# A mixture-of-experts block: the period loop written out, and expert weights requested ahead of their rows

## The reference

```
h = h + attn(layernorm(h))
x = layernorm(h)
topk_vals, topk_idx = top_k(x @ gate_w + gate_b, 2)
topk_w = softmax(topk_vals)
expert_out = relu(x @ w1[e] + b1[e]) @ w2[e] + b2[e]     # 16 experts, 64 -> 128 -> 64
h = h + layernorm(x + sum_k topk_w[k] * expert_out[topk_idx[k]]) * gamma + beta
```

## Time and profile before

| what | value |
|---|---|
| median of 3 runs | 4752.04 us (4744.88 to 4759.59) |
| profiled execution, its own time | 4752.51 us |
| its span, first to last instruction | 4750.7 us |
| mean granted TensorE clock | 0.839 |
| busy: PE, DVE, ACT, POOL | 77%, 63%, 46%, 70% |
| a steady period | 272.1 to 282.4 us |
| DMA over the span | 895.94 MB, mean 189 GB/s |

### The profile page before, as it was taken

How to read it: one execution, slowest core, us unless ns; L and a number is a source line. 1 busy time by engine, 2 the same in 40 slices (tenths; PEclk the granted TensorE clock), 3 DMA queues, 4 the chain that set the end, 5 groups by cost and what they waited for, 6 DMA issues and landing times.

```text
span 4750.7 us, 94109 instructions
## 1 busy us (share of the span) xinstructions
PE 3648.8 (77%) x24896; PEld 3139.7 (66%) x24896; DVE 3015.8 (63%) x9660; ACT 2167.0 (46%) x5266; POOL 3313.9 (70%) x3217
## 2 busy tenths in 40 slices
PE   4686887878778777877878887887878788788842
PEld 2565766767667676766767676775767677676732
DVE  1485858576684857767575775858577585767512
ACT  2354554444445444444544454454454445444401
POOL 0776777777677767777677776767777776777353
PEclk9888888888889888888988888898888978888855
DMA  7759584865848477584857758485774848562422
GB/s 238 247 154 273 160 266 132 253 190 181 244 126 267 131 234 218 164 256 119 258 146 238 222 161 246 125 262 148 221 237 141 259 125 267 151 177 58 120 66 62
DMA packets 922887, 895.94 MB, mean 189 GB/s; under 512 B 123866, under 2 KB 804442, under 8 KB 922200
## 3 DMA queue, kind: packets, MB, share of 16 engines
q1 hardware_dynamic: 785800, 577.28, 40.6%
q0 software_dynamic: 136528, 312.25, 22.0%
HBM read 562.75 MB, written 328.03 MB: 188 GB/s over the span
## 4 chain that ended last, share of the span: by engine, by line
PE 26%; issue 16%; DVE 16%; POOL 16%; DMA 9%; SPq 8%; ACT 7%; DVEq 1%; ACTq 0%; POOLq 0%
POOL ya L785 7%; POOL gath L753 7%; PE ps L862 4%; DMA xg<-xs_d 3%; PE ps L1005 3%; PE ps L876 3%; PE ps L1013 3%; POOL xs_d L769 3%; PE ps L807 2%; SPq L672 2%; PE ps L937 2%; SPq L699 2%; SPq L706 2%; DMA fm<-in_x 2%; SPq L700 1%
## 5 line engine op out<-in xcount | busy, mean ns | idle before, releaser
L753 POOL DMA_INDIRECT gath<-table,idx x2048 | 2107.0, 1029 | 885.9 <-issue 625.9
L785 POOL DMA_INDIRECT ya<-ys_d,row x576 | 585.5, 1017 | 343.5 <-issue 170.3
L1215 DVE TENSOR_TENSOR prod<-gath,corner_w 128x1024 f32<-128x1024 f32 x512 | 622.7, 1220 | 313.9 <-PE ps L862 186.9
L862 PE MATMUL ps<-const,prod 128*128 128x128 f32 x4096 | 628.3, 304 | 229.8 <-DVE prod L1215 211.8
L769 POOL DMA_INDIRECT xs_d<-xm,row x576 | 611.8, 1062 | 189.3 <-issue 173.2
L862 PEld LDWEIGHTS ps<-const,prod 128*128 128x128 f32 x4096 | 541.6, 159 | 265.9 <-issue 174.3
L876 PE MATMUL ps<-w_kv,samp_t 128*128 128x128 f32 x4096 | 634.4, 305 | 7.4 <-ACT kv_sb L1029 6.7
L876 PEld LDWEIGHTS ps<-w_kv,samp_t 128*128 128x128 f32 x4096 | 588.6, 219 | 68.5 <-issue 52.6
L959 PEld LDWEIGHTS ps<-v_sb,probs_t 128*128 128x128 f32 x2880 | 402.4, 212 | 165.7 <-DVE h L1223 75.8
L959 PE MATMUL ps<-v_sb,probs_t 128*128 128x64 f32 x2880 | 423.1, 293 | 112.6 <-DVE h L1223 69.5
L1029 ACT ACTIVATE rows<-ps 128x512 f32<-128x512 f32 x512 | 305.2, 596 | 428.5 <-PE ps L807 424.9
(11 more groups left out here) (162 smaller groups left out, 6156.4 us busy)
## 6 DMA issues: line engine op xcount, KB each, us to landing
table<-rows SPq DMA_DIRECT2D x224, 1024.0 KB
fm<-in_x SPq DMA_DIRECT2D x256, 512.0 KB
wx<-w_d SPq DMA_DIRECT2D x832, 128.0 KB
gath<-table,idx POOLq DMA_INDIRECT x2048
table<-rows SPq DMA_DIRECT2D x32, 960.0 KB
xg<-xs_d SPq DMA_DIRECT2D x208, 130.0 KB
ys_d<-yx SPq DMA_DIRECT2D x208, 128.0 KB
xs_d<-xm,row POOLq DMA_INDIRECT x576
```

The lines of the kernel that those rows point to most:

```text
L753: pool.indirect_dma_start(out=gath[:, n % NG, p, :], out_offset=None, in_=tables[par], in_offset=bass.IndirectOffsetOnAxis(ap=idx[:, par, ...
L785: pool.indirect_dma_start(out=ya[:, k, t, :], out_offset=None, in_=ys_d[par], in_offset=bass.IndirectOffsetOnAxis(ap=row[:, par, n:n + 1], ...
L862: last = pe.matmul(bank(0, p * P, p * P + P), prod[h][:, (p * 2 + dx) * P:(p * 2 + dx + 1) * P], ident, is_transpose=True, start=(dx == 0) ...
L1215: return dve.tensor_tensor(o, a, b, op)
```

## The change

Every period is written out: `drive` emits periods 0 to 14 one after the other with constants, so there is no loop, no jump back and no register sum ahead of a wait, and `Pair`, `settle` and `stretch` lose what served the loop. In `expert_load` the four `wx` transfers are now issued ahead of the group's `xg`. The wait for the scatter stands in group 0 alone, between its weights and its rows.

```diff
@@ drive
-            for k in range(LOOP_FROM):
+            for k in range(PAIRS - 1):
                 stretch(1 + k, None)
                 follow(engine, stages, k, Pair(k), k % 2)
-            with eng.Fori(0, (LOOP_TO - LOOP_FROM) // 2) as j:
-                for par in range(2):
-                    pair = Pair(LOOP_FROM + par, eng, j)
-                    stretch(LOOP, pair)
-                    follow(engine, stages, LOOP_FROM + par, pair, par)
-            for k in range(LOOP_TO, PAIRS - 1):
-                stretch(LOOP + 1 + k - LOOP_TO, None)
-                follow(engine, stages, k, Pair(k), k % 2)
-            stretch(LOOP + PAIRS - LOOP_TO, None)
+            stretch(PAIRS, None)
             follow_last(engine, stages)
@@ Pair
     def times(self, per, k=0):
-        if self.turn is None:
-            return self.off * per + k
-        if per not in self.products:
-            self.products[per] = self.eng.snap(self.turn * (2 * per))
-        return self.products[per] + (self.off * per + k)
+        return self.off * per + k
@@ expert_load
-                slot, turn = g % 2, g // 2 + 1
+                slot = g % 2
                 if g >= 2:
                     sp.wait_ge(*yx_sb.rise(pair, g - 1))
                 else:
-                    sp.wait_ge(*scattered.rise(pair, 16 * KT * SLOTS))
                     sp.wait_ge(*eid_ok.rise(pair, 1))
                     if begun(pair - 1):
                         sp.wait_ge(*yx_sb.rise(pair - 1, MG - g))
                     else:
                         sp.wait_ge(*experts_in.rise(Pair(0), 16 * FILLS))
-                sp.dma_start(xg[slot][:], xs_v[par][:, 4 * g:4 * g + 4, :]).then_inc(xg_in[slot].sem, 16)
                 for n in range(4):
                     j = 4 * g + n
                     e = sp.value_load(eid[j:j + 1, par:par + 1], min_val=0, max_val=E - 1)
                     sp.dma_start(wx[slot][:, n, :],
                                  w_d[bass.ds(e, 1)].rearrange("e p c -> p (e c)")).then_inc(wx_in[slot].sem, 16)
+                if g == 0:
+                    sp.wait_ge(*scattered.rise(pair, 16 * KT * SLOTS))
+                sp.dma_start(xg[slot][:], xs_v[par][:, 4 * g:4 * g + 4, :]).then_inc(xg_in[slot].sem, 16)
@@ settle (VectorE)
-                n = marks.get(thread[0], start[0])
-                if before[0] is None:
-                    dve.wait_ge(vec, n)
-                else:
-                    pair, head = before[0]
-                    dve.wait_ge(vec, pair.times(STEPS[LOOP], head + n))
+                dve.wait_ge(vec, marks.get(thread[0], start[0]))
```

More of the change, by code:

```diff
@@ L231 @@
 FIRST_PART = 3
-LOOP_FROM, LOOP_TO = 2, PAIRS - 2
-LOOP = 1 + LOOP_FROM
 TURNS = {
@@ L324, with __init__ @@
 class Pair:
-    def __init__(self, off, eng=None, turn=None):
-        self.off, self.eng, self.turn, self.products = off, eng, turn, {}
+    def __init__(self, off):
+        self.off = off
     def __add__(self, n):
-        p = Pair(self.off + n, self.eng, self.turn)
-        p.products = self.products
-        return p
+        return Pair(self.off + n)
     def __sub__(self, n):
@@ L580, in drive @@
                     stages[stage](Pair(0), 0, *args)
-            for k in range(LOOP_FROM):
+            for k in range(PAIRS - 1):
                 stretch(1 + k, None)
                 follow(engine, stages, k, Pair(k), k % 2)
-            with eng.Fori(0, (LOOP_TO - LOOP_FROM) // 2) as j:
-                for par in range(2):
-                    pair = Pair(LOOP_FROM + par, eng, j)
-                    stretch(LOOP, pair)
-                    follow(engine, stages, LOOP_FROM + par, pair, par)
-            for k in range(LOOP_TO, PAIRS - 1):
-                stretch(LOOP + 1 + k - LOOP_TO, None)
-                follow(engine, stages, k, Pair(k), k % 2)
-            stretch(LOOP + PAIRS - LOOP_TO, None)
+            stretch(PAIRS, None)
             follow_last(engine, stages)
-            stretch(LOOP + 1 + PAIRS - LOOP_TO, None)
+            stretch(PAIRS + 1, None)
         def first_of(pair):
-            return pair.turn is None and pair.off == 0
+            return pair.off == 0
         def begun(pair):
-            return pair.turn is not None or pair.off >= 0
+            return pair.off >= 0
         def unseen(n, pair):
@@ L1177, in _ @@
             marks = {}
-            before = [None]
             def step(ins):
@@ L1636, in _ @@
                    const[:, GY:GY + QT_N].unsqueeze(2).to_broadcast([P, QT_N, 2 * NP_]), ALU.add))
-            done = [None, 0]
             def stretch(n, pair):
-                last, count = done
                 assert not any(g.begun for g in staged), [g.begun for g in staged if g.begun]
[L1645 to L1655, removed]
                 start[0] = steps[0]
                 marks.clear()
-            setup_steps = steps[0]
             drive(dve, "vector", {"off_hidden": parts(off_hidden), "off_gelu": parts(off_gelu), "off_points": parts(off_points),
@@ L1666, in _ @@
                         "finish": parts(finish)}, stretch)
-STEPS = (34, 242, 334, 404, 404, 602)
 def kernel(**inputs):
```

## The result

The changed kernel takes 4775.5 us (median of 12 runs, 4761.7 to 4785.4) beside 4755.0 for the kernel before on the same chip (12 runs): ratio 1.0041, 95% interval 1.0029 to 1.0054. It is slower by 20 us, not by the 78 that were forecast. Its profiled execution spans 4765.9 us, beside 4750.7.

What follows compares the result with a forecast made beforehand. GpSimd, with 10 us left in a 277.7 us period, was taken to bound the kernel through its waits for `prod` and `ys_d`. Sum: 4752.5 - 17 (loop) + 97.5 (order) - 3 (group 0) = 4830 us; range 4763 to 4885.

Steps and rivals of the forecast that it cites:

- The loop: Writing out the periods removes five jumps back at 3.4 us each, 17 us gained; register sums counted as 0.
- rooms: Time TensorE now has between issue and turn of a group's rows: 6.33 us at group 2, 4.71 at group 11.
- part 2: Weights ahead of rows in groups 2 to 12: rows land later, 7.5 us a period in 13 periods, 97.5 us lost.
- D: Delay of the rows' issue on SP behind four weights: 4.5 us in groups 2 to 12, 3.75 at group 8.
- L: Time the rows take to land in the new order: taken as 3.5 us, between bounds of 1.75 and 4.78.
- Stalls of groups 3 to 7 up to some 3 us vanish in the 8.26 us.: New TensorE stalls at these groups cost nothing, absorbed by its present 8.26 us wait for group 8's rows.
- The rest at that for `ys_d`: Last store 5.8 us late: 2.5 shows at GpSimd's wait for `prod`, the remainder at its wait for `ys_d`.
- Group 0: Its weights ahead of the scatter's wait: 3 us gained behind the last scatter, 0 in steady periods.
- Rival 1: Rows land faster in the new order, in 1.75 us: 2.3 us a period, 30 in all, 4763 us; chance 0.17.
- rival 2: Rows' landing time stays at 4.78 us: 12.5 us a period, 163 in all, 4895 us; chance 0.17.
- rival 3: Rows wait only for a drained queue, so the order costs 0: faster, 4732 us; chance 0.11.
- rival 4: Small costs meet the gain: 1.5 us a period, 20 in all, no change; chance 0.05.

Runs made afterwards that it cites:

- body6: The kernel before with six periods in the loop's body instead of two, so one jump back instead of five, register sums kept: 4740.4 us, 0.9955.
- loop_vector: The kernel before with all engines' lists written out except VectorE's, whose loop stays: 4742.0 us, 0.9960 of the kernel before.
- sums_vector: rows_first with VectorE's register additions ahead of waits for its own results put back, without a jump: 4695.6 us, 0.9884 of the kernel before.
- w_2to7: rows_first with weights issued ahead of rows in groups 2 to 7 only: 4745.1 us, 0.9975 of the kernel before.
- rows_first: The changed kernel's written-out periods, but every group's rows issued ahead of its weights as in the kernel before: 4708.0 us, 0.9897 of the latter.
- g0_ahead: rows_first with only group 0's weights issued ahead of the wait for the scatter: 4698.2 us, 0.9868 of the kernel before.

## Why the prediction was wrong in size

The direction was right, and so was the forecast's picture of the order, with late rows and TensorE waiting for them. The size was not. By parts, taken in one sequence: 4755 - 49 (loop) - 14 (group 0) + 82 (order) = 4774, against 4775.5 measured. In the other sequence: 4755 + 103 (order and group 0, in the loop) - 84 (loop) = 4774. The forecast had - 17, + 97.5 and - 3.

- **The loop, 17 forecast, 49 to 84 measured. This is the step that failed.** It compared periods of the loop with and without a jump and took the second as the price of straight code: "so 3.4 us for each of five jumps: 17 us gained", with some 5 us as the bound for the rest. The difference of 3.4 is in the rows, but both kinds of period are longer than a written-out one, by 6.2 and 2.8. Jumps explain some 25 to 29 us (5 each by body6, 5.8 by loop_vector's VectorE alone), so even a jump costs more than 3.4. The rest, about 20, lies in periods without a jump. VectorE's additions are not it (sums_vector). Three things are left that no run separates: the sums on the four other engines, what a jump leaves behind in the next period, and the loading of longer instruction lists (3.67 + 2.74 MB with the loop, 3.34 + 1.76 written out), beside the clock that was named above. The period that was called straight-line in its second half, 279.30, still had its first half in the loop; one period's time was too thin a ground, since written-out periods range from 271.2 to 278.8.
- **The parts were added as if neither knew of the other.** The rooms of part 2 were read from the kernel with the loop, and there the order costs what was forecast, 103 us beside 94.5. Written out it costs 68. No term of the sum stood for that difference of 35 us, and its cause stays open.
- **By the rule of the Trainium skill** (Advanced Engine Details and Errata, Control Flow Timing), which gives a compare-and-branch about 108 ns, the jumps would by estimate have cost 0.5 us in all. The runs speak against this as a price of the loop: VectorE alone loses 3.50 us at a jump and the period 5.8. What the instruction takes by itself no run isolates.
- **The order, 97.5 forecast, 82 measured when written out.** D held: the rows are accepted later behind the transfer ahead of the group by 4.4 us at groups 2 and 12, 4.8 at 10 and 11, and 3.75 at group 8 (medians of twelve periods against those of before), where 4.5 and 3.75 were forecast. The term that was mis-sized is L, "I take 3.5". With the measured medians the same working gives group 2 4.5 + 2.70 - 6.33 = 0.9; group 8 3.75 + 3.09 - 4.78 = 2.1; group 10 4.5 + 3.17 - 6.72 = 0.9, so 3.0 together; group 12 4.5 + 3.50 - 6.03 = 2.0, so 5.0; in all 5.9 a period and 77 us in 13. Measured were 280.7 - 274.9 = 5.8 a period. This agrees so well partly by luck. The working takes its rooms from the kernel with the loop, and the pieces moved against each other: by the ratios groups 2 to 7 cost 37 instead of 22, the last groups 20 instead of 43.
- **"Stalls of groups 3 to 7 up to some 3 us vanish in the 8.26 us."** Wrong. The turn of group 5 waits 2.42 us (mean), and TensorE's wait at group 8 did not shrink by it (7.97 before, 8.90 after). w_2to7 prices groups 2 to 7 at 37 us. That SyncE's map loads and table writes follow TensorE and pass the delay on to group 8 fits this, but is argued.
- **"The rest at that for `ys_d`."** Wrong in place. The idle time ahead of fetches fell, by 19.3 us beside the kernel before and 11.8 beside rows_first, while that ahead of gathers grew by 63.2 and 90.1. My reading is that GpSimd arrives at the fetch later, behind the longer wait for `prod` (and a second one of 1.91 us eight gathers on, where 0.30 is usual), by more than the last store is late. The two waits lie in series on one engine, and the first takes what the second had.
- **Group 0, 3 forecast, 14 measured with 13 either way.** At the last scatter the first layer no longer waits for weights: it starts 4603.89 - 4602.09 = 1.8 us behind the turn, 4.4 before. In steady periods rows_first shows 1.5 us of such a wait a period and g0_ahead none. I had counted 0 there, and the sums of the twelve periods agree with that (3298.35 and 3298.65). Whether more than the 3 is gained is not resolved.
- **Rivals.** Rival 1 (L near 1.75) is refuted by the lags, though its time, 4763, was nearer; rival 2 (4.78) by the same lags; rival 3 by TensorE's waits; rival 4 (1.5 us a period) by 5.8. The measured time lies in the stated range, near its lower end, though the forecast's change of 78 us is almost four times the 20 measured. Nothing cancelled between the parts: 32 us too little for the loop, 15 too much for the order and 11 too little for group 0 all made the forecast too slow.

## What to carry to other kernels

A loop's price is not the difference between its turns with and without the jump. Here it was seen only by writing the periods out for all engines together, and freeing one engine showed almost none of it. Two changes that are made at once need not add up: each was worth a different amount with and without the other, so each part wants a run from both sides. Ahead of a transfer that the first consumer waits for, issue nothing that is used later; what can be asked for while its data is not ready, such as weights ahead of a wait for a scatter, cost nothing here and may have gained some us. When an engine's wait is followed back to one late transfer, try that transfer early before believing it, and look where the wait went: here 51 us of waiting for rows went, a new wait stood at the next group, and the period moved by little.

## What the runs showed of the hardware

- A jump back, in a loop on five engines: a stall at issue of 2.35 to 3.5 us on TensorE and 3.45 to 4.3 on VectorE (kernel before and body6), and a period longer by 3.4 us (all engines, beside periods of the loop), 5.8 (VectorE alone, with stalls of about 3.5) or 8.1 (a single period, one jump behind six periods).
- 4233 register additions on VectorE, each ahead of a wait, cost no measurable time (0.9884 beside 0.9897).
- A 130 KB transfer of rows was used 2.5 to 3.2 us after acceptance when it followed four transfers of weights (medians at groups 2, 8, 10 and 11 of the changed kernel, where TensorE waited for it in many periods), and 1.75 us in the quiet last stretch. Four transfers of weights, 128 KB each, with the value loads between them took 3.6 to 4.0 us of SyncE's queue in the rows shown, and 6.85 just behind table writes.
